# A vision-transformer layer on one core: the Haar synthesis as a column tree on GpSimd

## What is computed

```python
for _ in range(3):                                   # analysis
    cur, h, v, d = _dwt2(cur); details.append((h, v, d))
aw = sigmoid(cur.reshape(B, -1) @ Wa + ba)
rec = cur * aw[:, :, None]
for (h, v, d), (Wd, bd) in zip(reversed(details), det_params):   # synthesis, from coarse to fine
    flat = jnp.stack([h, v, d], axis=1).reshape(B, -1)
    w = softmax(flat @ Wd + bd, axis=-1)             # three gates per image and level
    rec = _idwt2(rec, h * w[:, 0], v * w[:, 1], d * w[:, 2])
# _split(x): ((x0 + x1) / sqrt(2), (x0 - x1) / sqrt(2)); _merge is its inverse; both along rows and columns
h = concat(cls_tok, rec)                             # 257 tokens of 256
h = h + attention(layernorm(h)); h = h + ffn(layernorm(h))
```

## Time and profile before

| | |
|---|---|
| device time, three runs | 1749.71, 1754.5, 1755.43 us (median 1754.5) |
| span of the profiled execution, first to last instruction | 1750.5 us; the page has no other time for it |
| busy, share of the span | PE 95%, DVE 84%, ACT 76%, POOL 64% |
| one image's period in the middle of the run | 49.27 us (from 794.31 to 843.58) |
| granted TensorE clock | 0.976 as a mean, 1.00 from 170 to 1650 us |

### The profile page before, as it was taken

One profiled execution on the slowest core, in us unless ns is written; L12 is line 12 of the kernel. 1 busy time (PEld: TensorE's weight loads), 2 busy tenths in 40 slices (PEclk: granted clock), 3 DMA queues, 4 the chain that ended last, 5 costly groups with the idle time before them and its releaser, 6 DMA issues.

```text
span 1750.5 us, 48653 instructions
## 1 busy us (share of the span) xinstructions
PE 1664.2 (95%) x16742; PEld 1278.3 (73%) x16742; DVE 1470.0 (84%) x4972; ACT 1323.6 (76%) x3812; POOL 1120.1 (64%) x1034
## 2 busy tenths in 40 slices
PE   7758999999999999999999999999999999999975
PEld 6635777777777777777777777777777777777653
DVE  3837888899888888899888888899888888889874
ACT  0326888888888888888888888888888888888762
POOL 0087667766777666766777667666677667666500
PEclk9789999999999999999999999999999999999986
DMA  9311111111111111111111111111111111111100
GB/s 320 110 61 61 56 53 56 53 67 57 61 68 68 59 61 57 50 65 62 56 68 68 66 55 60 54 56 66 55 64 68 68 53 61 56 53 62 44 7 13
DMA packets 90168, 113.70 MB, mean 65 GB/s; under 512 B 14818, under 2 KB 52163, under 8 KB 89667
## 3 DMA queue, kind: packets, MB, share of 16 engines
q1 hardware_dynamic: 89922, 110.59, 18.1%
HBM read 26.62 MB, written 8.42 MB: 20 GB/s over the span
## 4 chain that ended last, share of the span: by engine, by line
PE 88%; DVE 4%; SPq 3%; POOL 2%; ACT 1%; issue 1%; DMA 0%; DVEq 0%; POOLq 0%; ACTq 0%
PE bank L725 45%; PE bank L842 9%; PE bank L983 7%; PE bank L831 6%; PE bank L829 6%; PE bank L994 3%; PE bank L853 3%; PE bank L903 3%; PE bank L891 2%; PE bank L1003 2%; SPq L320 1%; PE bank L882 1%; DVE arena L1283 1%; PE bank L950 0%; POOL rot L486 0%
## 5 line engine op out<-in xcount | busy, mean ns | idle before, releaser
L482 POOL TENSOR_TENSOR arena<-rq,cos 128x512 f32<-128x512 f32 x256 | 326.1, 1274 | 280.0 <-ACT rq L526 280.0
L535 ACT ACTIVATE arena<-arena,nm 128x129 f32<-128x129 f32 (+1 forms) x1024 | 455.6, 455 | 0.0
L486 POOL TENSOR_TENSOR rot<-rot,sin 128x512 f32<-128x512 f32 x256 | 326.3, 1275 | 103.9 <-DMA rot<-rq 103.9
L725 PE MATMUL bank<-xt_h,weights 128*128 128x256 f16 x2048 | 378.9, 273 | 9.2 <-ACT rq L526 7.8
L526 ACT ACTIVATE rq<-bank,bqk 128x256 f32<-128x256 f32 x512 | 214.4, 471 | 170.1 <-PE bank L725 155.3
L1283 DVE CUSTOM_DVE_ANT_0 arena<-bank,bias 128x129 f32<-128x129 f32 (+1 forms) x1024 | 317.9, 352 | 26.5 <-issue 16.6
L489 POOL TENSOR_TENSOR arena<-arena,rot 128x512 f32<-128x512 f32 x256 | 314.2, 1228 | 37.3 <-POOL rot L486 0.9
L1291 DVE TENSOR_TENSOR ptr_l<-bank,ptr_h 128x384 f16<-128x384 f32 x512 | 280.0, 552 | 31.8 <-ACT ptr_h L545 29.4
L545 ACT ACTIVATE ptr_h<-bank 128x384 f16<-128x384 f32 x512 | 249.1, 486 | 68.6 <-PE bank L725 44.0
L725 PE MATMUL bank<-xt_l,weights 128*128 128x256 f16 x1024 | 279.6, 273 | 0.0
L842 PE MATMUL bank<-eye,arena 128*128 128x128 f32 x1536 | 253.0, 277 | 8.5 <-DVE ptr_l L1291 4.4
(11 more groups left out here) (200 smaller groups left out, 3182.5 us busy)
## 6 DMA issues: line engine op xcount, KB each, us to landing
rot<-rq SPq DMA_DIRECT2D x512, 128.0 KB, 2.0
arena<-in_x SPq DMA_DIRECT2D x4, 2048.0 KB, 15.2
xin<-in_x SPq DMA_DIRECT2D x32, 256.0 KB, 2.8
hr<-hr SPq DMA_DIRECT2D x32, 256.0 KB, 2.3
out<-h SPq DMA_DIRECT2D x64, 128.0 KB, 2.1
arena<-in_L_attn_w_qkv SPq DMA_DIRECT2D x2, 1536.0 KB, 8.6
weights<-in_L_ffn_w_down SPq DMA_DIRECT2D x1, 1024.0 KB, 11.8
arena<-in_L_ffn_w_gate SPq DMA_DIRECT2D x1, 1024.0 KB, 8.5
```

Source lines behind the costliest of these rows:

```text
L482: pool.tensor_tensor(dst, rq[:, g % 2].rearrange("p j (t n) -> p j t n", t=T), cos[:, :].rearrange("p (t n) -> p t n", t=T).unsqueeze(1).b ...
L486: pool.tensor_tensor(r, r, sin[:, :].unsqueeze(1).broadcast_to([P, 2, SIDE]), ALU.mult).then_inc(t2_ready, 1)
L535: act.activation(cols, cols, ACT.Exp, bias=nm[:, t, h:h + 1], scale=-1.0, accum_out=rs[:, t, h:h + 1]).then_inc(e_done, 1)
L725: ins = pe.matmul(dst, lhs[l], rhs[r], start=start and n == 0, stop=stop and n == len(parts) - 1)
```

## The change

The synthesis is now done as a full column Haar tree. GpSimd makes the sums and the differences of neighbouring columns at all three levels, in a tile `haar` of 256 + 128 + 64 + 64 = 512 columns. TensorE applies one row operator to each of the four parts, into four parts of `b_bank` (`coarse` is gone, and so is its use of `u_bank`). ScalarE's `synthesis_out` (in `coarse_out`'s place) copies the 512 columns to `syn`. GpSimd's new `image_back` runs the tree back in six instructions (`quad_sum`, `pair_sum`, `hh`), each of which writes every second column, and the last one raises `h_ready`. VectorE's `image_out` is gone; its list is otherwise the same. Projection 5 waits for `syn_out_done` in place of `h_ready`. The raw image's next load may start when the first level has read the image. The tables of patterns and factors in the preparation are built anew for 16 factors per image in place of 12.

```diff
@@ GpSimd
+            def column_step(low, high, src):
+                pool.tensor_tensor(high, src[:, :, 0::2], src[:, :, 1::2], ALU.subtract)
+                return pool.tensor_tensor(low, src[:, :, 0::2], src[:, :, 1::2], ALU.add)
+            def column_bands(first):
+                d1, d2, d3, low = columns(haar)
+                column_step(s1[:, :, :], d1, xin).then_inc(coeffs, 1)
+                pool.wait_ge(coeffs, first)
+                column_step(s2[:, :, :], d2, s1).then_inc(coeffs, 1)
+                pool.wait_ge(coeffs, first + 1)
+                column_step(low, d3, s2)
             def row_operators(a):
...
-                pool.wait_ge(coarse_ready, a)
                 pool.tensor_copy(op_now[:, :, :], ops[:, bass.ds(a, 1), :, :].rearrange("p a o r -> p (a o) r")).then_inc(coeffs, 1)
                 pool.wait_ge(x_in, 16 * (a + 1))
-                pool.tensor_tensor(s1[:, :, :], xin[:, :, 0::2], xin[:, :, 1::2], ALU.add).then_inc(coeffs, 1)
...
+                column_bands(3 * a + 1)
+                build_rowop(op_now[:, :, :])
+            def image_back(a):
+                if not image(a) or begun and a == 0:
+                    return
+                d1, d2, d3, low = columns(syn)
+                pool.wait_ge(syn_out_done, a + 1)
+                pool.tensor_tensor(quad_sum[:, :, 0::2], low, d3, ALU.add)
+                pool.tensor_tensor(quad_sum[:, :, 1::2], low, d3, ALU.subtract).then_inc(back, 1)
+                pool.wait_ge(back, 2 * a + 1)
+                pool.tensor_tensor(pair_sum[:, :, 0::2], quad_sum[:, :, :], d2, ALU.add)
+                pool.tensor_tensor(pair_sum[:, :, 1::2], quad_sum[:, :, :], d2, ALU.subtract).then_inc(back, 1)
+                pool.wait_ge(back, 2 * a + 2)
+                if a:
+                    pool.wait_ge(hr_ready, a)
+                    pool.wait_ge(xn_ready, a)
+                pool.tensor_tensor(hh[:, :, 0::2], pair_sum[:, :, :], d1, ALU.add)
+                pool.tensor_tensor(hh[:, :, 1::2], pair_sum[:, :, :], d1, ALU.subtract).then_inc(h_ready, 1)
@@ GpSimd's step(s)
                 rotate(s + 1, 5)
+                image_back(s + 2)
+                rotate(s + 1, 6)
                 image_rstd(s + 2)
-                rotate(s + 1, 6)
                 rotate(s + 1, 7)
@@ ScalarE
-                act.activation(pair_sum[:, :, :].rearrange("p t n -> p (t n)"), u_bank[:, 0:SIDE], ACT.Copy).then_inc(coarse_out_done, 1)
+                act.activation(syn[:, :], b_bank[:, :], ACT.Copy).then_inc(syn_out_done, 1)
@@ TensorE
-                pe.matmul(b_bank[:, :], rowop[:, 0, :], xin[:, :, :].rearrange("p t n -> p (t n)"), start=True, stop=True).then_inc(syn_ready, 1)
-            def coarse(a):
...
+                for o, (dst, src) in enumerate(zip(columns(b_bank), columns(haar))):
+                    ins = pe.matmul(dst.rearrange("p t n -> p (t n)"), rowop[:, o, :], src.rearrange("p t n -> p (t n)"), start=True, stop=True)
+                ins.then_inc(syn_ready, 1)
             def project(b, g):
...
-                    pe.wait_ge(h_ready, b + 2)
+                    pe.wait_ge(syn_out_done, b + 2)
@@ VectorE's step(s)
-                image_out(s - 1)
                 evict_scores(s - 3, 8)
                 evict_scores(s - 3, 9)
                 weights_lo(s - 3, 6)
                 image_stats(s - 1)
                 evict_scores(s - 3, 10)
                 attended_lo(s - 3, 0)
```

More of the change, by code:

```diff
@@ L1006, in _ @@
             synthesise(0)
-            coarse(0)
             pe.wait_ge(turned_copied, 4)
@@ L1035, in step @@
                 project(s, 4)
-                coarse(s + 1)
                 scores(s - 1, 4)
@@ L1404, in values_lo @@
                 stt(vl[b % 2][:, v // 2, cols], b_bank[:, :], 1.0 / WSCALE, vh[b % 2][:, v // 2, cols], ALU.mult, ALU.subtract).then_inc(vl_done, 1)
-            def image_out(a):
-                if not image(a) or begun and a == 0:
-                    return
-                dve.wait_ge(syn_ready, a + 1)
-                dve.wait_ge(coarse_out_done, a + 1)
-                if a:
-                    dve.wait_ge(hr_ready, a)
-                tt(hh[:, :, :].rearrange("p t (n r) -> p t n r", r=2), b_bank[:, :].rearrange("p (t n r) -> p t n r", t=T, r=2),
-                   pair_sum[:, :, :].unsqueeze(3).broadcast_to([P, T, 128, 2]), ALU.add).then_inc(h_ready, 1)
             def image_stats(a):
```

113 lines of the change are left out of this document (41 added, 72 removed).

## The result

| | before | after |
|---|---|---|
| device time, median of four runs (lowest to highest) | 1754.77 us (1749.71 to 1755.43) | 2140.91 us (2138.16 to 2141.06) |
| ratio, 95% interval | | 1.2205 [1.218, 1.223] |
| span of the profiled execution | 1750.5 us | 2136.3 us |
| one image's period, the one shown from the middle of the run | 49.27 us | 61.44 us |
| one image's period, mean of 29 (image 2 to image 31) | 49.08 us | 61.56 us |

The kernel became slower by 386 us; 2118 us (2045 to 2190) was forecast. The windows of one period, in the columns of the earlier trace rows: the whole period, TensorE's stop in it, and the time right behind the stop.

The account below looks back on a forecast made before the run. TensorE's work was taken to bound the kernel before. A new loop of 59.05 us plus 2.2 for the clock gave +12.0 thirty times (360); with 4 for preparation, 1750.5 became 2114.5, or 2118 us on the runs' scale (2045 to 2190).

Parts of the forecast that it names:

- The deciding step: GpSimd finishes `hh` behind rotation 5, ten microseconds after VectorE's statistics ask; TensorE stands before head 8: loop 59.05 us, +9.8 per image.
- release to copy of projection 3, at full clock, and clock: TensorE's release at head 8 to ScalarE's copy of projection 3: 37.45 us, plus 2.2 for half speed after the stop.
- copy to the end of rotation 5: ScalarE's copy of projection 3 to GpSimd's end of rotation 5: 14.77 us, plus 0.4 for the later projection 5.
- statistics to release, with hand-overs: VectorE's statistics to the end of the attended low part: 3.58 us, plus two engine hand-overs of 0.1 each.
- VectorE's lateness: Unknown price: VectorE comes out of its stop 0.3 us late against TensorE, 0 to 0.5 us.
- "clock stays up" rival: TensorE's clock doesn't fall after its stops: only +9.8 us per image, 2052 us; chance 12%.
- The tree back: GpSimd's six `image_back` instructions, priced at the same widths' 0.29, 0.40 and 0.62 us: 2.65 us in the loop.
- The bound of twice: Upper price of GpSimd's `image_back` for writing every second column: twice as long, +2.65 us per image.
- TensorE's saving: Synthesis on TensorE falls from 2.36 to 1.1 us: 1.26 us per image, 40 us over 32 images, if nothing else happened.
- The start: Preparation up to the first image's statistics, with larger tables and awaited row operators: +4 us (0 to 8).
- GpSimd's busy time: Sign of being right: GpSimd's busy time up by about 32 x 3.9 = 125 us.
- the rival "faster": `hh` complete less than 0.35 us after VectorE's statistics ask, so TensorE's saving stands: 40 us less, 1715; chance 2%.

Follow-up runs that it names:

- experiment 1: Kernel before, plus a one-column GpSimd memset behind rotation 5 that VectorE's image statistics wait for, and image_rstd moved behind rotation 6: 2029.33 us, ratio 1.1578.
- experiment 2: Changed kernel with VectorE's image statistics moved from behind the split of head 6 to behind the eviction of head 14: 1856.38 us, ratio 1.0587.
- experiment 4: Changed kernel with GpSimd's image_back ahead of rotation 5 instead of behind it: 1968.42 us, ratio 1.123.
- experiment 6: Changed kernel with six more GpSimd instructions of the tree back's widths, results unused, ahead of image_back for every image but the first: 2247.48 us, ratio 1.282.
- experiment 8: Changed kernel with image_back ahead of rotation 4, image_rstd behind rotation 5, and ScalarE rounding the tokens before copying the synthesis; statistics at their old place: 1829.12 us, ratio 1.0436.
- experiment 9: Experiment 8 with TensorE's list reordered: transposes of head 6, synthesis, values 4 and 5, then transposes of the quantised tokens: 1825.49 us, ratio 1.0413.
- experiment 5: Changed kernel with 64 unused f16 matmuls of 256 columns on TensorE between projection 6 and the transposes of head 8: 2126.17 us, ratio 1.2128.
- experiment 7: Experiment 3 with six more GpSimd instructions of the tree back's widths, results unused, ahead of image_back for every image but the first: 1824.94 us, ratio 1.041.
- experiment 3: Experiment 2 with ScalarE also rounding the tokens before it copies the 512 synthesised columns: 1813.54 us, ratio 1.0345.
- experiment 11: Kernel before with the coarse part cut to its first matmul, so synthesis levels 2 and 3 are missing: 1749.43 us, ratio 0.9975.
- experiment 12: Experiment 11 with ScalarE rounding tokens before the coarse copy and TensorE doing values 4 and 5 before the tokens' transposes: 1749.17 us, ratio 0.9984.
- experiment 10: Experiment 9 with VectorE's statistics behind head 10's eviction and the attended low part, and ScalarE's head 6 weights ahead of the quantised tokens: 1822.34 us, ratio 1.039.

## Why the prediction held, and where it was off

**The deciding step is shown.** `hh` complete behind rotation 5, VectorE's statistics stuck in front of everything, TensorE released late, the next projections late: experiment 1 makes the loop with a memset alone, experiment 2 breaks it by moving one call, experiment 4 shortens it by what the loop says, and experiment 6 lengthens it by that and 1.1 us more, partly of clock. In experiments 8 and 9 it closes once more, with rotations 4 and 5 taken out of it.

**The terms of the sum**, forecast and measured in the period shown:

| step | forecast, us | measured, us |
|---|---|---|
| release to copy of projection 3, at full clock, and clock | 37.45 + 2.2 | 38.98 (804.87 to 843.85) |
| copy to the end of rotation 5 | 14.77 + 0.4 | 15.8 (to 859.65) |
| `image_back` | 2.65 | 3.0 (859.65 to 862.64) |
| statistics to release, with hand-overs | 3.58 + 0.2 | 3.67 (862.64 to 866.31) |
| period | 61.25 | 61.44 |

- *That the period came out within 0.2 us is in part luck.* The clock was taken 0.7 too high, the way to rotation 5 0.6 too low, the tree 0.3 too low, and these cancel. Each of the 30 releases begins at 0.50, as forecast, and TensorE stays there for 3.7 us, about as long as after the shorter of the two stops of the earlier trace rows. By the table this costs 1.5 us, but only 1.2 of it is the clock: in experiment 5, in the rounds at full clock, the stretch takes 37.74 to 37.85 us, and 37.75 in experiments 8 and 9. The 0.3 above 37.45 stays at full clock. The prediction had it among its unknown prices as VectorE's lateness (0 to 0.5) and at nothing in the sum. The "clock stays up" rival is excluded by the windows.
- *The tree back* costs 3.0: 0.32, 0.46 and 0.73 us for 64, 128 and 256 columns, where reading every second column costs 0.29, 0.40 and 0.62. The bound of twice was far off. Writing every second column is not what costs the difference: the extra instructions of experiments 6 and 7 do so too and take 0.29 to 0.30, 0.40 and 0.61 to 0.62 us; they read one part twice, the tree reads two. Which property counts was not isolated.
- *From the copy of projection 3 to rotation 5* it took 1.0 us more than before, where 0.4 was allowed. It arises at the transposes of the quantised tokens: 6.81 us behind the copy (843.85 to 850.66) instead of 5.83 (841.13 to 846.96), since ScalarE waited 1.02 us for the synthesis and rounded after it.
- *TensorE's saving* is 1.05 us, not 1.26 (1.31 against 2.36): the trace has two records for each f32 matmul, and in experiment 3 one takes 0.27 us for 64 columns as for 128, and 0.43 for 256; in the period shown there the passes of 64 columns mostly start 0.11 us apart, like those of 128. So the pieces of 64 cost what 128 columns cost.
- *The start* was given 4 us and took 10.2. Part of it may be no effect of the change: the first image landed at 51.23 us instead of 44.93, but in experiment 1, whose preparation is that of the kernel before, it landed late too (50.19) and the first synthesis was at 78.8 (73.7 before, 77.4 after).
- *The run as a whole* came out 22 us above the 2114.5 of the sum. Of that the start is 6. Another 6 arise since the growth was counted from a period of 49.27 us, where the mean is 49.08 (30 x 0.19), and 9 since the mean period is 61.56 and not 61.25 (30 x 0.31).
- *GpSimd's busy time* rose by 130.5 us (125 forecast), the mean clock fell to 0.903 (0.9), and the stops are at the transposes of head 8: as stated. They are 30, since the last of the 31 waits in the view is one of 2.3 us in the emptying pipeline.

**What the prediction read wrongly without harm to its number.** It opened with "TensorE sets the pace, by work and not by waits", and gave the rival "faster" 1715 us if `hh` came in time. Experiments 11 and 12 show that 0.87 us less work per image brings 0.13 to 0.14. Behind TensorE's full row two other limits stand within half a microsecond: ScalarE's rounding (0.5 us of slack, 846.45 against 846.96) and VectorE's list around the statistics. A busy share of 99.9% says that TensorE has no gaps; it doesn't say that TensorE's work is the shortest way round. So most of the saving couldn't have been cashed even with a perfect hand-over; this is inferred from the cut in the kernel before. The same misreading stands in the expectations of experiments 2 and 3, which were 71 and 67 us too low at their upper ends. Those of experiments 8 and 9 (44 and 60 too low) took the loop for gone, that of experiment 10 (32 too low) took VectorE's list for the bound.

**What stays open.** Experiments 3, 8, 9 and 10 have lists in four different orders and periods mostly between 50.7 and 51.0 us. In 8 and 9 the loop through rotation 3 makes them, as shown. In 3 and 10 that loop is open; their stops are named above, but which loop makes their periods was not isolated. No order tried makes the tree as fast as the kernel before: the best is 1813.54 us, 3.45% slower.

## What to carry to other kernels

When work is handed to another engine, ask first where in that engine's list it will be done and at what point in the consumer's list it is awaited; a hand-over of no work at all cost 16% here, and moving one call gave back three quarters of the loss. Before counting on less work for an engine that is busy all the time, look at how early its inputs arrive: with 0.5 us of slack at one input, even the best periods of experiment 11 gained only 0.4 of 0.87 us. Read it over many periods, not one. Follow a stall until it meets itself; if it does, it is paid in every round and can be summed before anything runs.

## What the hardware showed that was not expected

- Two of VectorE's TENSOR_SCALAR instructions on f32 in SBUF are held when they start beside a GpSimd instruction. The variance of two elements takes 0.17 us alone; beside one it ends 0.02 to 0.03 us behind GpSimd's end, after up to 1.27 us. The normalisation of 256 columns takes 0.41 alone and ends 0.15 us behind GpSimd's end, after 0.66 and 1.36 us (experiment 3). Those of one element aren't held: in experiment 11, 271 of them ran beside a GpSimd instruction of over 1 us, and none took over 0.3 us. By the Trainium skill (SBUF — State Buffer, Who interferes with whom), `tensor_scalar` can take ports that VectorE shares with GpSimd, and whoever comes first holds them for the whole instruction. The traces agree for the two widths. The start decides: recorded 0.01 us behind GpSimd's the variance went through in experiment 11, 0.02 behind it was held, and 0.4 us of a period hangs on that. The prediction had this in the 1.26 us of the earlier trace rows, but as a constant.
- Short stops of TensorE can cost more than their length: in experiment 2 stops of 0.4, 1.4 and 1.1 us per image go with a fall of the clock in every third or fourth period, which adds 1.5 to 2 us to it; in experiment 3, with 0.4, 0.4 and 1.1 us, the middle of the run shows no such periods.
